# Routed experts in pairs of 128-row units: 72 pairs of two experts in place of 80 pairs of one

## The reference

```python
weights, indices = _gate(xt, gate_w)      # softmax; best 2 of 4 groups; best 4 of 16 experts
c = zeros((T, 16)).at[arange(T)[:, None], indices].add(weights)
h1 = einsum('td,edi->tei', xt, w1)        # each expert: 256 -> 128
h3 = einsum('td,edi->tei', xt, w3)
y = einsum('tei,eid,te->td', silu(h1) * h3, w2, c)
z = silu(xt @ ws1) * (xt @ ws3) @ ws2
x = layernorm(x + y + z)
```

## Time and profile before

| | us |
|---|---|
| runs of the kernel (3) | 562.92 median, 561.91 to 564.67 |
| the profiled execution, its own time | 563.45 |
| its span, first to last instruction | 561.6 |
| TensorE matmul busy | 457.2 (81%) |
| TensorE weight load busy | 320.5 (57%) |
| VectorE busy | 395.1 (70%) |
| ScalarE busy | 291.8 (52%) |
| GpSimd busy | 293.1 (52%) |

### The profile page before, as it was taken

How to read it: one execution, slowest core, us unless ns; L and a number is a source line. 1 busy time by engine, 2 the same in 40 slices (tenths; PEclk the granted TensorE clock), 3 DMA queues, 4 the chain that set the end, 5 groups by cost and what they waited for, 6 DMA issues and landing times.

```text
span 561.6 us, 12184 instructions
## 1 busy us (share of the span) xinstructions
PE 457.2 (81%) x3189; PEld 320.5 (57%) x3213; DVE 395.1 (70%) x1147; ACT 291.8 (52%) x627; POOL 293.1 (52%) x334
## 2 busy tenths in 40 slices
PE   1599979794979796976995899899889899898930
PEld 1145636442546454543553789789777777787620
DVE  1454686874685764667687677668979989888754
ACT  3154564544462634361221477676766776777621
POOL 1001010578767676765774000057778787777771
PEclk9999999997999997987998999999999999999985
DMA  8121314364433121222753477699999999898651
GB/s 210 53 63 51 95 36 114 83 207 144 151 111 107 64 103 67 103 76 104 253 213 114 124 220 211 199 250 305 302 279 305 274 332 316 275 313 292 193 201 50
DMA packets 55012, 97.74 MB, mean 174 GB/s; under 512 B 8752, under 2 KB 22080, under 8 KB 54976
## 3 DMA queue, kind: packets, MB, share of 16 engines
q1 hardware_dynamic: 29472, 38.56, 23.3%
q0 software_dynamic: 12288, 33.57, 19.3%
q10 hardware_dynamic: 13216, 25.17, 12.1%
HBM read 50.88 MB, written 46.40 MB: 173 GB/s over the span
## 4 chain that ended last, share of the span: by engine, by line
PE 37%; DVE 21%; DMA 12%; issue 11%; POOL 8%; ACT 7%; ACTq 1%; SPq 1%; DVEq 1%; POOLq 0%
DMA wa_stage<-expert_out,result_of 5%; POOL expert_in L391 4%; PE h_even L1142 3%; PE h_odd L1142 3%; PE h_even L1144 3%; PE h_odd L1144 3%; PE h_odd L1143 3%; DMA q_fm<-expert_out,result_of 3%; DVE x_all L1096 3%; PE h_even L1143 3%; DMA expert_out<-k_exp 3%; PE h_even L1188 2%; PE t L1367 2%; ACT x_all L490 2%; PE t L1149 2%
## 5 line engine op out<-in xcount | busy, mean ns | idle before, releaser
L391 POOL DMA_INDIRECT expert_in<-x_all,slots x128 | 133.2, 1041 | 45.7 <-issue 35.8
L416 POOL DMA_INDIRECT wa_stage<-expert_out,result_of x64 | 63.9, 998 | 19.1 <-issue 14.2
L416 POOL DMA_INDIRECT q_fm<-expert_out,result_of x32 | 31.5, 984 | 76.1 <-DMA expert_out<-k_exp 66.9
L377 POOL TENSOR_SCALAR neg_mean<-mv 128x4 f32<-128x4 f32 x16 | 5.3, 329 | 109.3 <-DVE mv L714 109.0
L645 ACT ACTIVATE wa_hi<-bias_heads 128x256 f16<-128x256 f32 x80 | 33.2, 415 | 33.5 <-DVE bias_heads L1079 33.0
L1367 PE MATMUL t<-ident,kv 128*128 128x128 f32 x320 | 48.1, 273 | 1.6 <-DVE xsT_lo L1068 1.6
L1068 DVE TENSOR_TENSOR xsT_lo<-t,xsT_hi 128x512 bf16<-128x512 f32 x60 | 41.0, 684 | 11.8 <-ACT xsT_hi L597 11.0
L597 ACT ACTIVATE xsT_hi<-t 128x512 f16<-128x512 f32 x60 | 35.5, 593 | 24.4 <-PE t L1367 12.2
L1143 PE MATMUL h_even<-xsT_lo,we_hi 128*128 128x256 bf16 x160 | 43.6, 273 | 0.0
L1142 PE MATMUL h_even<-xsT_hi,we_hi 128*128 128x256 f16 x160 | 43.6, 273 | 0.0
L1144 PE MATMUL h_even<-xsT_hi,we_lo 128*128 128x256 f16 x160 | 43.6, 273 | 0.0
(11 more groups left out here) (231 smaller groups left out, 1435.3 us busy)
## 6 DMA issues: line engine op xcount, KB each, us to landing
kv<-expert_in SPq DMA_DIRECT2D x80, 256.0 KB, 4.6
expert_out<-k_exp ACTq DMA_DIRECT2D x40, 256.0 KB
expert_out<-q_exp ACTq DMA_DIRECT2D x40, 256.0 KB
stage<-in_L_ffn_w SPq DMA_DIRECT2D x48, 128.0 KB
expert_in<-wa_stage SPq DMA_DIRECT2D x17, 256.0 KB
x_in<-in_L_attn_x SPq DMA_DIRECT2D x8, 512.0 KB, 4.3
out<-gated ACTq DMA_DIRECT2D x8, 512.0 KB, 4.3
expert_in<-x_all,slots POOLq DMA_INDIRECT x128, 2.4
```

What stands on the lines that cost most here:

```text
L391: pool.indirect_dma_start(xs_dram, bass.IndirectOffsetOnAxis(ap=slots[:, b, t, j:j + 1], axis=0), x_all[:, b, t, :], None).then_inc(dispat ...
L416: pool.indirect_dma_start(y_got[i][:, j, :], None, ys_dram[0:pairs_until(k) * PAIR, :], bass.IndirectOffsetOnAxis(ap=result_of[:, b, t, j: ...
```

## The change

The constants, and the shape of a pair:

```diff
-LIST_AT = 320
-SUM_FROM = 3
-GATHER_FROM = 21
-GATHER_HEAD = 12
+LIST_AT = 0
+POS_AT = 320
+SUM_FROM = 2
+GATHER_FROM = 14
+GATHER_HEAD = 8
+PACKED = 6
...
-    PAIR = 2 * P
-    MOST = NB * S // PAIR
-    NPAIR = NT * TOP_K // 2 + E
+    UNIT = P
+    PAIR = 2 * UNIT
+    MOST = NB * S // UNIT
+    NUNIT = NT * TOP_K + E
+    NPAIR = NUNIT // 2
```

SyncE reads one number per pair that holds both units' blocks, and issues a DMA of 128 KB for each:

```diff
-                row = sp.value_load(pair_row[0:1, p, :], min_val=0, max_val=SLOTS - PAIR)
+                both = sp.value_load(pair_row[0:1, p, :], min_val=0, max_val=2 ** 20 - 1)
+                blocks = (both >> 10, both & 1023)
...
-                sp.dma_start(xs[r][:, :, :], rows_of(xs_dram, row)).then_inc(xs_loaded[r], 16)
+                for u, number in enumerate(blocks):
+                    sp.dma_start(xs[r][u * UNIT // 2:(u + 1) * UNIT // 2, :, :], rows_of(xs_dram, number * UNIT)).then_inc(xs_loaded[r], 16)
```

TensorE: the experts of six units are in one number. A loop of 8 pairs reads four numbers, the first at its head and one after `up_pair` of its pairs 0, 3 and 6, and takes 20 experts out of them (16 of its own and the last 4 of the loop before). `up_pair` runs on 128 columns per unit, `down_pair` takes each unit's own weights, and the transposes write every second column:

```diff
+                    to = t_bank[r % 2][:, c * PAIR:(c + 1) * PAIR].rearrange("p (n i) -> p i n", i=2)
...
-            def chunk_of(g):
-                return pe.value_load(pair_chunk[0:1, g, :], min_val=SHARED, max_val=NCH - 1)
+            def chunks_of(k, q2):
+                n = min(PACKED, 20 - PACKED * k)
+                six = pe.value_load(six_experts[0:1, k, q2, :], min_val=0, max_val=E ** PACKED - 1)
+                return [pe.snap((six >> 4 * i & E - 1) + SHARED, min_val=SHARED, max_val=NCH - 1) for i in range(n)]
...
                 for k in range(2):
-                    for c in range(KC):
-                        cols = slice((c * 2 + k) * INTER, (c * 2 + k + 1) * INTER)
-                        last = product(h_banks[r % 2][0][:, k * PAIR:(k + 1) * PAIR],
-                                       we_hi[:, chunk, cols], we_lo[:, chunk, cols],
-                                       xsT_hi[r][:, c, :], xsT_lo[r][:, c, :], c == 0, c == KC - 1)
+                    for u in range(2):
+                        tok = slice(u * UNIT, (u + 1) * UNIT)
+                        for c in range(KC):
+                            cols = slice((c * 2 + k) * INTER, (c * 2 + k + 1) * INTER)
+                            last = product(h_banks[r % 2][0][:, k * PAIR + u * UNIT:k * PAIR + (u + 1) * UNIT],
+                                           we_hi[:, chunks[u], cols], we_lo[:, chunks[u], cols],
+                                           xsT_hi[r][:, c, tok], xsT_lo[r][:, c, tok], c == 0, c == KC - 1)
...
-                w2_hi, w2_lo = we_hi[:, chunk, W13:], we_lo[:, chunk, W13:]
...
+                for u in range(2):
+                    tok = slice(u * UNIT, (u + 1) * UNIT)
+                    last = product(y_bank[r % 2][:, u * D:(u + 1) * D], aT_hi[r % 2][:, tok], aT_lo[r % 2][:, tok],
+                                   we_hi[:, chunks[u], W13:], we_lo[:, chunks[u], W13:], True, True)
...
+                chunks = chunks_of(0, q2)
                 for i in range(2 * RING):
...
-                    up_pair(g, r, chunks[i])
-                    if i < 2 * RING - 1:
-                        chunks.append(chunk_of(g + 1))
...
+                    up_pair(g, r, chunks[4 + 2 * i:6 + 2 * i])
+                    if i % 3 == 0:
+                        chunks += chunks_of(i // 3 + 1, q2)
+                    if i >= 2 or late(q2, 1):
+                        down_pair(g - 2, (r - 2) % RING, chunks[2 * i:2 * i + 2])
```

```diff
+                if part == 0:
+                    dve.wait_ge(slots_ready, NB)
+                    dve.wait_ge(starts_placed, 1)
+                    dve.tensor_tensor(in_last, of_tiles, placed(0), ALU.is_gt).then_inc(place_step, 1)
+                if part == 1:
+                    dve.wait_ge(shifts_placed, 1)
+                    dve.tensor_tensor(in_last, in_last, placed(1), ALU.mult).then_inc(place_step, 1)
+                if part == 2:
+                    dve.wait_ge(shifts_placed, 2)
+                    dve.scalar_tensor_tensor(moved, of_tiles, 2.0, placed(0), ALU.mult, ALU.add).then_inc(place_step, 1)
...
...
```

Parts 5 to 8 take the eight largest of each tile as before, two batches each, and part 9 makes the indices. All ten parts run beside `shared_hidden` 7 to 11; none is left in the pairs. TensorE waits for `place_step` 3 before it transposes the first pair. In the loops `combine` is shifted by one: the last two combines of a batch come in the first pair of the next loop, and the two of batch 6 after the pairs:

```diff
-                    add = [(b, i // 2, 2 * (i % 2) + j) for j in range(2)] if b is not None else ()
+                    add = ()
+                    if i == 0 and b is not None and late(b, 1):
+                        add = [(b - 1, TT - 1, 2 + j) for j in range(2)]
+                    elif i > 0 and b is not None:
+                        add = [(b, (i - 1) // 2, 2 * ((i - 1) % 2) + j) for j in range(2)]
...
+            for j in range(2):
+                combine(summed - 1, TT - 1, 2 + j)
```

More of the change, by code:

```diff
@@ L847, in plan_pairs @@
                     dve.tensor_reduce(cand_pos[:, :], cand_rank[:, :, :], AX_X, ALU.add).then_inc(plan_step, 1)
+                    dve.wait_ge(plan_step, 5)
+                    dve.tensor_scalar(cand_whole[:, :], cand_pos[:, :], 1.5, 0.5, ALU.subtract, ALU.mult).then_inc(plan_step, 1)
+                    for k in range(CANDS):
+                        last = dve.tensor_scalar(cand_at[k], unit_no, cand_pos[:, k:k + 1], None, ALU.is_equal)
                 if part == 3:
-                    dve.wait_ge(plan_step, 5)
@@ L898, in place_results @@
[L898 to L905 removed]
+                    dve.wait_ge(place_step, 1)
@@ new lines, in place_results @@
+                    dve.wait_ge(shifts_placed, 1)
[3 more added lines that the diff above has]
+                    dve.scalar_tensor_tensor(moved, of_tiles, 2.0, placed(0), ALU.mult, ALU.add).then_inc(place_step, 1)
+                if part == 3:
+                    dve.wait_ge(place_step, 3)
+                    dve.tensor_tensor(moved, moved, in_last, ALU.add).then_inc(place_step, 1)
@@ L906, in place_results @@
+                if part == 4:
+                    dve.wait_ge(place_step, 4)
+                    dve.tensor_tensor(of_tiles, moved, sel_all[:, :, :, :].rearrange("p b t e -> p (b t) e"),
+                                      ALU.mult).then_inc(place_step, 1)
+                if 5 <= part < 9:
+                    dve.wait_ge(place_step, 5)
+                    first = 2 * (part - 5)
                     for b in range(first, first + 2):
@@ L1002, in _ @@
             dve.memset(begun[:, :, 0:1], 0.0)
+            dve.tensor_copy(place_lo, place_weights[0:3 * E, :].unsqueeze(2).to_broadcast([3 * E, 4, P]))
+            for k in range(CANDS):
+                dve.tensor_scalar(pos_of_cand[:, k, 2 * E:], expert_of_cand, cand_number[:, k:k + 1], None, ALU.mult)
             batch(0, False, False, True, early=0)
@@ L1052, in _ @@
             plan_pairs(4)
+            plan_pairs(5)
             shared_hidden(7)
+            place_results(0)
             add_shared(2)
-            placed = 0
-            for n in range(4, EARLY):
+            shared_hidden(8)
+            for part in range(1, 4):
+                place_results(part)
+            shared_hidden(9)
+            for part in range(4, 6):
+                place_results(part)
+            add_shared(3)
+            shared_hidden(10)
+            for part in range(6, 8):
+                place_results(part)
+            shared_hidden(11)
+            for part in range(8, 10):
+                place_results(part)
+            add_shared(4)
+            for n in range(6, EARLY):
                 for g in range(SHARED * n, SHARED * (n + 1)):
                     shared_hidden(g)
-                    for part in range(placed, placed + 3):
-                        place_results(part)
-                    placed += 3
                 add_shared(n - 1)
@@ L1228, in rank_candidates @@
                     pe.matmul(rank, ones[:, :], begun[:, k:k + 1, 0:NT].to_broadcast([P, CANDS, NT]), start=False, stop=False)
-                pe.matmul(rank[:, 1, :], ones[:, :], first_in[:, 0, :], start=False, stop=True).then_inc(ranked, 1)
+                for k in range(CANDS - 1):
+                    last = pe.matmul(rank[:, k + 1:, :], ones[:, :], first_in[:, k:k + 1, :].to_broadcast([P, CANDS - 1 - k, NT]),
+                                     start=False, stop=k == CANDS - 2)
+                last.then_inc(ranked, 1)
             def list_pairs():
@@ L1353, in _ @@
             up(7, 3, 1)
+            place_blocks()
             down(2)
-            for n in range(4, EARLY):
+            up(8, 4, 0)
+            place_before()
+            up(9, 4, 1)
+            down(3)
+            for n in range(5, EARLY):
                 up(SHARED * n, n, 0)
@@ L1447, with _plan_constants @@
         "L0_ffn_w3", "L0_ffn_ws1", "L0_ffn_ws2", "L0_ffn_ws3"]
-def _plan_constants(np, batches, pairs_of_batch, experts):
-    most, pairs = batches * pairs_of_batch // TOP_K, batches * pairs_of_batch + experts
+def _plan_constants(np, batches, blocks_of_batch, experts):
+    most, units = batches * blocks_of_batch // TOP_K, batches * blocks_of_batch + experts
     blocks = most + 1
```

217 lines of the change are left out of this document (111 added, 106 removed).

## The result

The changed kernel takes **625.22 us** (median of 4 runs, 623.92 to 625.75) against 563.79 us for the kernel before in the same comparison (561.91 to 567.88, 4 runs): a ratio of 1.108, 95% interval 1.101 to 1.114. It is slower by 61 us; 605 were forecast, in a range of 585 to 655. The profiled run took 625.28 us, its span is 623.3.

A forecast was written before the change was run, and what follows sets the result against it. TensorE's sequencer, with its array also at the limit in plain pairs, was taken as the bound. 563.45 + 42.5 (pairs) + 1.0 (tail) - 1.5 (plan) = 605.5, forecast as 605 us, range 585 to 655.

The forecast's parts named there:

- The bound: Pairs: TensorE's sequencer and array both at their limit in plain pairs; sequencer alone in each loop's first two pairs.
- The missing 0.10 us: Pairs of the kernel before: sequencer sum 2.57 us against 2.67 measured; the difference put on reads, 0.86 us each.
- up_pair: Up products on 128 columns: eight register groups instead of four, 8 x 0.24 = 1.90 us a pair, 0.95 more.
- Reads: Expert reads in the pairs: 4 per 8 pairs instead of 10, 0.43 us a pair, 0.65 less.
- taking the experts out: Shift, mask, addition and copy in registers for 20 units in 8 pairs: 0.40 us a pair.
- The rival of 1.0 to 1.6 us: Taking experts out unfused or each value checked: pairs of 4.2 to 4.8 us, 650 to 690 us total; chance 0.18.
- down_pair: Down products: a second fused and a second ALU instruction, 0.36 + 0.22 = 0.58 us a pair; array work stays.
- The sum: Sequencer's time for one changed pair: 3.59 us; 72 pairs take 258.5 us, 42.5 us more than before.
- The tail: Behind the pairs: two combines more at 0.5 us each, +1.0 us.
- The plan: Fewer VectorE `place_results` steps before the pairs: -1.5 us, between 0 and -2.1, limited by the last dispatch and first load.
- 312 to 314: Sign expected in the trace after: the first up matmul comes at 312 to 314 us.
- eight pairs fewer: 72 pairs instead of 80: worth 8 x 2.67 = 21 us at the present rate, and 4 MB off DMA.

The follow-up runs named there:

- e1b_constant_undisturbed: Changed kernel with constants for the pairs' experts (no reads, shifts, masks or register addresses), on a 564 us chip: 554.6 us, ratio 0.982 to the kernel before.
- e9_reads_one_by_one: Changed kernel with each unit's expert read by itself, 20 reads in 8 pairs instead of 4, no shift and mask: 715.2 us, ratio 1.266 to the kernel before.
- e3_last_combines_first: Changed kernel with batch 6's last two combines moved ahead of the shared network's last batch on VectorE: 652.5 us, ratio 1.038 to the kernel before.
- e7_before_shift_mask: Kernel before with expert numbers stored times 32 and taken out by shift and mask: 642.0 us, ratio 1.019 to the kernel before.
- e1_constant_experts: Changed kernel with constants for the pairs' experts (no reads, shifts, masks or register addresses), on a 630 us chip: 618.6 us, ratio 0.979 to the kernel before.

## Why the prediction was right, and where it was off

- **The bound.** Right: TensorE's sequencer sets the pace of the changed pairs. Its steps there have near constant lengths, a pair falls from 3.74 to 2.72 us when reads and register work go (`e1b_constant_undisturbed`), and rises by 1.27 where the sequencer's sum gives 1.22 (`e9_reads_one_by_one`). For the kernel before it was right up to the gathers only. I had averaged 2.67 us over all 80 pairs; they are 2.51 and then 2.78 to 2.81, and in the second stretch taking the read gaps away changes 0.03 us. The traces point to GpSimd's chain of gathers there, with DMA at 0.91 to 0.93 beside it. The missing 0.10 us that I put on the reads belongs in part to that.
- **`up_pair`:** 1.90 us forecast, 1.97 measured. Right; the array has 1.34 us to do there, as the constants show.
- **Reads:** 0.43 forecast, 0.50 measured, and **taking the experts out:** 0.40 forecast, 0.44 measured. Shift and mask are not fused, but single instructions of 0.098 us: 36 in 8 pairs, two for each of the 20 units that a loop names, less the four that stand lowest in their value and need no shift. My nearest row was of fused arithmetic, so the term came out near by luck: the addition and the copy that I had counted have no instruction of their own. The rival of 1.0 to 1.6 us is out: between 400 and 540 us there are 18 loads and 18 asserts, so no new value has a check.
- **`down_pair`:** 0.58 forecast, 0.60 measured.
- **The sum:** 3.59 against 3.80 us (3.78 over all 72 pairs): 72 x 0.19 = 13.7 us of the 20 that I was short, spread over all terms.
- **The tail:** +1.0 forecast, +9.8 measured. This is the term that failed. I priced the two combines that stand behind the pairs at VectorE's 0.5 us each and did not ask who waits for them: `rstd_of` of batch 6 on GpSimd, and behind it eight gathers. Moving them gave 9.4 us back (`e3_last_combines_first`).
- **The plan:** -1.5 forecast, with -2.1 as its end; -4.2 measured. The last dispatch itself came earlier, and the first load with it: 301.7 in place of 304.5. I had held it fixed, and so the first `up` came at 310.13 us, ahead of the 312 to 314 that I named as a sign. Which edit moved the dispatch was not tried. The end of the middle in the kernel after:

```profile
298.29 0.97 POOL L404 DMA_INDIRECT expert_in<-x_all,slots  x1 [0.30 <-issue]
301.71 8.66 SPq L340 DMA_DIRECT2D kv<-expert_in  x9
305.22 0.63 PE L1441 MATMUL t<-ident,kv 128*128 128x128 f32 x4 [2.02 <-DMA kv<-expert_in]
```

The three errors, 13.7 + 8.8 - 2.7 us, are the 19.8 between 605.5 and the 625.3 of the profiled run. They do not all point the same way: the plan's 2.7 us hides a part of the rest. Where the gain of eight pairs fewer went is answered by the kernel with constants: units of 128 rows with no reads and no register work take 555 us, below the kernel before, and with them 626. These 71 us are what the sequencer's work costs the changed kernel; the kernel before pays for such work too, so 555 us is not what the units alone are worth.

## What to carry to other kernels

Add up what an engine's sequencer issues in a loop (starts of its register, load, branch and wait instructions, not their durations) and set it against the array's work before cutting tiles finer: here each group with an expert in a register costs 0.24 us, at 256 columns and at 128 alike. Then look at the steps one by one: a sequencer at its limit has even ones, and one that waits has some that are long. A step moved in one engine's order is priced by who waits for it, not by its own duration: two combines of half a microsecond each cost 9.4 us. And where two stretches of a loop differ in who runs beside it, average neither the period nor the bound over both.

## What the runs showed of the hardware

- In the pairs of the kernel after (400 to 520 us) a shift or a mask in a register holds TensorE's sequencer 0.098 us where its record is 36 ns, and a fused instruction and the ALU instruction after it at least 0.124 and 0.112, with records of 46 and 32. A load of the packed number from SBUF holds it 0.36 to 1.1 us.
- In the pairs of `e9_reads_one_by_one` TensorE is busy for 139.6 of 208 us and the granted clock is 0.83, so part of the stretch runs at 1.2 GHz in place of 2.4; the changed kernel, busy for 181.9 of 211.6 us, has 1.00 there. The lower clock hardly shows in the time: 89 us more against the 88 that were expected without it.

```profile
450.00:658.00 208.00, 139.64 (x1368) 123.25 (x1367) 101.40 (x269) 83.69 (x182) 86.56 (x101) 0.83 0.54 164
```

- On chips 15 and 9 the kernel before takes 66 us more than on 4 and 11. In `e7_before_shift_mask`, whose first 300 us are those of the kernel before, every engine is within about 0.5 us of its time up to the first indirect DMAs of GpSimd, near 105 us; from there on all engines have stalls that the profile puts down to no engine of the core (it says `remote`, or names nothing), the longest from 119 to 126 us:

```profile
118.78 0.38 PE L1144 MATMUL h_even<-wa_hi,xT_lo 128*128 128x512 f16 x1 [0.31 <-issue]
...
125.85 0.29 DVE L745 TENSOR_REDUCE logits<-t 128x64 f32<-128x128 f32 x1 [13.13 <-remote]
```

VectorE has the same stall of 13.1 to 13.2 us in `e1_constant_experts` and `e3_last_combines_first`, on both of these chips, and not in the traces of the other two. No run looked into its cause, and it stays open, as does whether it belongs to the chips or to the hour at which they were used. The pairs of `e3_last_combines_first`, bound by the sequencer, show none of it.
